# A four-layer graph network on one core: the third layer's normalisation moved from ScalarE to GpSimd and VectorE

## What is computed

```python
def _layernorm(x, axis=-1, eps=1e-05):
    m = jnp.mean(x, axis=axis, keepdims=True)
    v = jnp.var(x, axis=axis, keepdims=True)
    return (x - m) / jnp.sqrt(v + eps)
...
    h = jnp.maximum(_layernorm(x, axis=-1), 0.0)
    x = x + _L0_gnn_ref(h, adj, L0_gnn_W, L0_gnn_a)
    h = jnp.maximum(_layernorm(x, axis=-1), 0.0)
    x = x + _L1_gnn_ref(h, adj, L1_gnn_eps, L1_gnn_W1, L1_gnn_b1, L1_gnn_W2, L1_gnn_b2)
    h = jnp.maximum(_layernorm(x, axis=-1), 0.0)
    x = x + _L2_gnn_ref(h, adj, L2_gnn_weight, L2_gnn_bias)
    h = jnp.maximum(_layernorm(x, axis=-1), 0.0)
    x = x + _L3_gnn_ref(h, adj, nodemask, L3_gnn_weight, L3_gnn_w_ih, L3_gnn_w_hh, L3_gnn_b_ih, L3_gnn_b_hh)
```

## Time and profile before

| | us |
|---|---|
| median of 3 runs | 711.43 |
| lowest and highest | 709.85 and 711.65 |
| the profiled execution | 711.34 |
| its span, first to last instruction | 709.6 |
| of it, `first_layers` | about 336 |
| one steady slot | 18.02 |

### The profile page before, as it was taken

How to read it: one execution, slowest core, us unless ns; L and a number is a source line. 1 busy time by engine, 2 the same in 40 slices (tenths; PEclk the granted TensorE clock), 3 DMA queues, 4 the chain that set the end, 5 groups by cost and what they waited for, 6 DMA issues and landing times.

```text
span 709.6 us, 13197 instructions
## 1 busy us (share of the span) xinstructions
PE 659.9 (93%) x4380; PEld 430.4 (61%) x4380; DVE 601.8 (85%) x1361; ACT 524.3 (74%) x962; POOL 401.1 (57%) x356
## 2 busy tenths in 40 slices
PE   1899999999999999983899999999999999999995
PEld 1678888888888888862455555555454555555552
DVE  3677777777777787666699999999999999999996
ACT  1588888888888888732477888777777777877774
POOL 4556666666666666521255555555555555555554
PEclk9999999999999999986899999999999999999998
DMA  5111111111111100000343333333333333333332
GB/s 154 31 31 31 31 31 31 30 31 31 31 30 31 30 16 1 2 0 1 59 61 60 60 61 65 68 76 75 75 61 75 74 76 75 61 75 69 69 72 74
DMA packets 114690, 35.82 MB, mean 50 GB/s; under 512 B 87680, under 2 KB 114624, under 8 KB 114624
## 3 DMA queue, kind: packets, MB, share of 16 engines
q1 hardware_dynamic: 114624, 34.98, 23.3%
HBM read 9.80 MB, written 4.19 MB: 20 GB/s over the span
## 4 chain that ended last, share of the span: by engine, by line
DVE 36%; issue 9%; PE 3%; POOL 2%; ACT 1%; DMA 0%; DVEq 0%; POOLq 0%; SPq 0%
DVE h_parts L1286 12%; DVE cand L1293 7%; DVE t_parts L1278 6%; DVE r L1297 5%; DVE new L1282 4%; PE psum L50 3%; POOL h0T L1253 2%; DVE out L1269 2%; DVE h_parts L1288 0%; DMA h_nodes<-h_parts 0%; DVEq L1296 0%; ACT cand L1230 0%; POOLq L1035 0%; PE psum L1182 0%; ACT z L1225 0%
## 5 line engine op out<-in xcount | busy, mean ns | idle before, releaser
L50 PE MATMUL psum<-h_parts,gru_w 128*128 128x512 f16 x720 | 185.1, 382 | 6.1 <-DVE out L1269 3.6
L1253 POOL TENSOR_TENSOR h0T<-cand,zh 128x512 f32<-128x512 f32 x80 | 101.6, 1270 | 142.8 <-DVE cand L1293 142.8
L50 PE MATMUL psum<-t_parts,gru_w 128*128 128x512 f16 x720 | 181.5, 379 | 0.0
L50 PEld LDWEIGHTS psum<-h_parts,gru_w 128*128 128x128 f16 x720 | 69.9, 98 | 91.6 <-issue 10.6
L1247 POOL TENSOR_TENSOR zh<-z,h0T 128x512 f32<-128x512 f32 x80 | 101.7, 1272 | 26.2 <-ACT z L1225 26.2
L50 PEld LDWEIGHTS psum<-t_parts,gru_w 128*128 128x128 f16 x720 | 67.1, 98 | 66.2 <-DVE t_parts L1278 2.3
L1222 ACT CAST t_parts<-psum 128x512 f16<-128x512 f32 x80 | 46.8, 585 | 73.1 <-PE psum L50 73.1
L1286 DVE CAST h_parts<-h0T 128x512 f16<-128x512 f32 x80 | 90.1, 1126 | 4.8 <-PEq L373 4.8
L572 POOL TENSOR_TENSOR prob<-prob,row_max 128x512 f32<-128x512 f32 x64 | 68.7, 1087 | 19.7 <-DVE row_max L947 18.5
L1230 ACT ACTIVATE cand<-new,gates_b 128x512 f32<-128x512 f32 x80 | 65.0, 812 | 6.7 <-DVE new L1282 6.6
L913 DVE BATCH_NORM_STATS2 stats<-x_all 128x6 f32<-128x128 f32 x256 | 55.5, 279 | 13.9 <-DMA x_all<-in_x 8.9
(11 more groups left out here) (131 smaller groups left out, 1202.2 us busy)
## 6 DMA issues: line engine op xcount, KB each, us to landing
x_all<-in_x SPq DMA_DIRECT2D x16, 256.0 KB, 3.2
adj<-in_adj SPq DMA_DIRECT2D x16, 256.0 KB, 2.8
out_x<-out SPq DMA_DIRECT2D x16, 256.0 KB, 2.3
h_nodes<-h_parts SPq DMA_TRANSPOSE x80, 3.1
gw<-in_L_gnn_weight SPq DMA_DIRECT2D x1, 320.0 KB, 4.7
W<-in_L_gnn_W SPq DMA_DIRECT2D x2, 128.0 KB, 4.6
wi<-in_L_gnn_w_ih SPq DMA_DIRECT2D x1, 192.0 KB, 4.9
wh<-in_L_gnn_w_hh SPq DMA_DIRECT2D x1, 192.0 KB, 5.0
```

The costliest lines, as they stand in the source:

```text
L50: return nc.tensor.matmul(out, lhsT, rhs, start=start, stop=stop)
L1253: pool.tensor_tensor(state(now), by_graph(cand[now.s][:, :]), by_graph(zh[now.s][:, :]), ALU.add)\
```

## The change

For layer 2 the activations and the shift go. POOL gets a new function `centre`, which subtracts the mean on the whole 128x512 tile, at the very start of its slot, ahead of `add_self`. DVE gets `normalise_2` where `shift_of(at(3), 2)` stood: it waits for `centred[2]` and for `rstd_ready[2]`, and then does four `tensor_scalar` of 128x128, in place on `y[2]`, each of which multiplies by the graph's `rstd` and takes the maximum with 0. ACT still makes `rstd`. Layer 1's normalisation stays as it was under new names (`normalise_1`, `shift_of_1`).

```diff
@@ -586,11 +586,21 @@
+            def centre(group, n):
+
+                wait_apart(var_ready[n], group.count)
+                if group.before(1).exists:
+                    wait_apart(z_psum[n - 1], group.before(1).count)
+                pool.tensor_tensor(y[n][:, :, :], xs(group), mean_var[n][:, :, 0:1].to_broadcast([128, GROUP, DIM]),
+                                   ALU.subtract).then_inc(centred[n], 1)
+
             def slot(at, number):
                 if number == 1:
                     score_weights.pick_rows(pool)
                 if number == 2:
                     pool.wait_ge(gru.layers_loaded, gru.all_layers_loaded)
+                if at(3):
+                    centre(at(3), 2)
                 if at(2):
                     add_self(at(2))
                 if at(3):
...
-            def normalise(group, n):
-
-                wait_apart(shift_ready[n], group.count)
+            def normalise_1(group):
+
+                wait_apart(shift_ready, group.count)
                 for g in range(GROUP):
-                    last = a.activation(y[n][:, g, :], t["x"][:, group.graph(g), :], ACT.Relu,
-                                        bias=shift[n][:, g:g + 1], scale=rstd[n][:, g:g + 1])
-                last.then_inc(y_ready[n], 1)
+                    last = a.activation(y[1][:, g, :], t["x"][:, group.graph(g), :], ACT.Relu,
+                                        bias=shift[:, g:g + 1], scale=rstd[1][:, g:g + 1])
+                last.then_inc(y_ready[1], 1)
...
                 if at(2):
                     rstd_of(at(2), 2)
-                    normalise(at(2), 2)
                 if at(3):
                     keep_h0T(at(3))
...
+            def normalise_2(group):
+
+                dve.wait_ge(centred[2], group.count)
+                dve.wait_ge(rstd_ready[2], group.count)
+                for g in range(GROUP):
+                    last = v.tensor_scalar(y[2][:, g, :], y[2][:, g, :], rstd[2][:, g:g + 1], 0.0, ALU.mult, ALU.max)
+                last.then_inc(y_ready[2], 1)
...
                 if at(3):
-                    shift_of(at(3), 2)
+                    normalise_2(at(3))
                 if number == GROUPS + 2:
                     gru.scale(dve)
                     gru.split(dve)
```

More of the change, by code:

```diff
@@ L388, in first_layers @@
         rstd = [one(f"rstd{n}", [128, GROUP]) for n in LAYERS]
-        shift = {n: one(f"shift{n}", [128, GROUP]) for n in (1, 2)}
+        shift = one("shift", [128, GROUP])
         y = [one(f"y{n}", [128, GROUP, DIM]) for n in LAYERS]
@@ L414, in first_layers @@
         rstd_ready = [sem(f"rstd_ready{n}") for n in LAYERS]
-        shift_ready = {n: sem(f"shift_ready{n}") for n in (1, 2)}
+        shift_ready = sem("shift_ready")
         y_ready = [sem(f"y_ready{n}") for n in LAYERS]
-        centred = {n: sem(f"centred{n}") for n in (0, 3)}
+        centred = {n: sem(f"centred{n}") for n in (0, 2, 3)}
         gone_ready = sem("gone_ready")
@@ L864, in slot @@
                 if at(2):
-                    normalise(at(2), 1)
+                    normalise_1(at(2))
                 if at(1):
@@ L920, in moments, with shift_of_1 @@
                 last.then_inc(var_ready[n], 1)
[L922 to L925, removed]
+            def shift_of_1(group):
+                dve.wait_ge(rstd_ready[1], group.count)
+                v.scalar_tensor_tensor(shift[:, :], mean_var[1][:, :, 0], -1.0, rstd[1][:, :], ALU.mult, ALU.mult)\
+                    .then_inc(shift_ready, 1)
+            def normalise_2(group):
[4 more added lines that the diff above has]
+                last.then_inc(y_ready[2], 1)
             def find_gone(group):
@@ L998, in slot @@
                 if at(2):
-                    shift_of(at(2), 1)
+                    shift_of_1(at(2))
                 if at(0):
```

## The result

The changed kernel takes 748.0 us (median of 4 runs, 747.22 to 748.14) against 711.54 before: a ratio of 1.0506, with a 95% interval of 1.0489 to 1.0524. It is slower, as forecast, but by 36 us and not by 22, and it lies above the upper end of the range, 739. The profiled execution took 747.22 us, with a span of 745.4.

What follows compares the result with a forecast made beforehand. A loop of DVE's chain plus PE's own work was taken to bound the kernel; 13 steady slots x 1.54 = 20.0 us plus 1.75 at the end gave 21.8, so 733.1 us from 711.34, range 729 to 739.

Steps and rivals of the forecast that it cites:

- The bound: Steady slot: DVE's chain of 6.89 us plus PE's own 11.13 us sets its length of 18.02 us.
- ACT worth nothing: ACT's four removed activations, 1.65 us per slot, lie outside the loop and were costed at 0.
- POOL's subtraction and `add_self`: POOL's slot start: subtraction 0.27 us after bn_aggr, 1.04 long; add_self follows with 0.04 overlap, runs 1.26, ends at 194.35.
- The standstill: DVE's first scaling is blocked while POOL's add_self runs and ends 0.07 us after it, at 194.42.
- the rival in which DVE gets in between: DVE's first scaling starts as POOL's subtraction ends, so add_self waits: 0.50 us per slot, 718.0 us; chance 0.09.
- The scalings: DVE's other three scalings follow each other at 0.14 us each, 0.42 for three, between 0.08 and 0.20.
- d: Lengthening of DVE's chain, and so of each steady slot: 1.54 us, with bounds of 1.26 and 1.90.
- The clock: PE's granted clock falls in its longer pause, 1.7 us per slot; held only as a rival, chance 0.07.
- The rival's 746 us: PE's clock falling in every third slot, about 3 us each, adds some 13 us: 746 us; chance 0.07.
- The tail: Slots 16, 17 and 18 at the end add 0.8, 0.85 and 0.1 us, 1.75 together; the GRU itself is untouched.

Runs made afterwards that it cites:

- with PE filled: The changed kernel with seven added float32 matmuls of 128x128 on PE between layer 2's aggregation and the scores: 739.27 us, ratio 1.0397.
- the delayed kernel before: The kernel before with nine bn_stats of a constant tile into scratch behind the shift on DVE: 746.94 us, ratio 1.0503.
- both kernels rearranged: Changed kernel with DVE's moments ahead of the scalings and add_self behind POOL's bias, 713.28 us; kernel before with add_self behind the bias, 706.64 us.

## Why the prediction was right and where it was wrong

**The bound: right.** A loop through DVE's chain and PE's own work set the slot, with a wait of 0.18 us as its only trace. A delay put into that chain in the kernel before reproduced the loss (746.94 us), and taking the shift's standstill out of it made the kernel faster. The loop had more room in it than the row showed: 0.45 us of pause, not 0.18. The prediction's sentence "making it shorter gives back at most the 0.18" was wrong for that reason.

**ACT worth nothing: right.** Putting the activations back left the time at 748.2.

**POOL's subtraction and `add_self`: right,** to 0.01 us: the start 0.27 after the variance, 1.04 long, `add_self` right behind, the end at 0.04 less than the sum of both.

**The standstill: right.** The first scaling ended 0.09 us after `add_self` (210.62 + 1.28 = 211.90 against 211.81), where 0.07 was forecast, and it disappeared when `add_self` was moved. The Trainium skill (SBUF — State Buffer, "Who interferes with whom") has the rule that whoever issues first gets the shared ports for the whole instruction. The trace agrees in each of slots 3 to 17, where the four scalings are shown as 1.86 or 1.87 us and `add_self` starts first; the rival in which DVE gets in between did not occur in any. With POOL idle, in the kernel that moved `add_self`, the four took 0.88 us.

**The scalings: mis-sized.** The term was 0.14 from start to start; measured was 0.195 to 0.20. I had gone halfway between a `bn_stats` and a `bn_aggr`, for two numbers at a time. That is what the form with a constant takes, 0.13 to 0.14 from start to start, but a scale from SBUF adds 0.06 to each, for which there was no unblocked row. With it d is 1.74 instead of 1.54, and the steady slots lose 2.6 us more.

**The clock: the step that failed.** The sum has no term for the clock. The prediction had its fall as a rival with a chance of 0.07, and read from slot 2 that a gap of 0.93 us did not fell the clock. The new pause was twice as long, and no row of the kernel before covered it; that was no ground to hold the clock up and put the term at nothing. In place of nothing it was five falls and about 8 us, the largest part of the miss. The price of a fall was put at 3 us, from a stretch of 6.5 us at the lower level; here it stayed low for 3.4 us and cost 1.6. The rival's 746 us came near by luck: its 13 us for the clock were too many, on top of a sum that was too small elsewhere.

Across the runs the falls go with the pause. With pauses of 0.2 to 0.7 us per slot (as the rows show them) there was none, with 1.1 to 1.4 none, with 1.35 to 1.66 none, and with 1.92 to 2.29 (three kernels) there were five among the steady slots. Which slots it hits is not decided by the length of the pause: most pauses of 1.95 us had no fall, and neither had the longest, 2.29. What decides it stays open.

**The tail: too small.** The forecast had 1.75 us for slots 16 to 18 and nothing after them. The same milestones in both kernels:

| milestone | before, us | after, us | later by |
|---|---|---|---|
| scores of slot 3 | 52.32 | 54.15 | 1.83 |
| scores of slot 15 | 268.54 | 298.24 | 29.70 |
| scores of slot 16 | 286.22 | 318.38 | 32.16 |
| `add_attended` of slot 17 | 302.31 | 335.60 | 33.29 |
| first copy of the GRU's weights | 311.06 | 345.18 | 34.12 |
| first cast of the GRU | 336.49 | 371.22 | 34.73 |
| end of the span | 709.6 | 745.4 | 35.8 |

The chain is 1.83 up to slot 3's scores and 12 x 1.74 = 20.9 up to slot 15's, together 22.7. The four falls in that stretch are 6.46. Two slots without a fall, 8 and 15, are 0.28 us longer than the others, 0.56 together, and so are two slots of the kernels with `add_self` moved and with PE filled; the cause is not shown. From slot 15's scores to slot 16's it is 2.46 more, for the fifth fall and slot 16 itself. The two were not separated in this kernel. In the delayed kernel before, which had no fall there, this slot lost 0.69, and by that the fall cost about 1.8. From slot 16's scores to the GRU it is another 2.57 us. In slot 17 the transposes of the GRU's weights run at the lower clock, which they did not before. In slot 18 the scalings delay the GRU's scale operations by 1.46 us (357.83 against 322.25, less the 34.12), and with the block on the split gone 0.61 of it stays. The last 1.1 us arise within the GRU, which the change does not touch. Its start runs at the lower clock in both kernels; after its first cast that lasts about 7.5 us before and 8.7 after. At half the clock 1.2 us more cost at most 0.6, so this could be half of the 1.1 us, and it was not tried; the rest is open.

The sum then is 22.7 + 6.46 + 0.56 + 2.46 + 2.57 + 1.07 = 35.8 us, the difference of the two spans (745.4 - 709.6). Since the milestones come from the same traces, the sum must come out; what it shows is where the time went. Of the 14 us that the forecast of 21.8 lacks, about 8 are the clock, 2.6 the scalings in the steady slots, and some 3.3 the two longer slots and the tail.

## What to carry to other kernels

An engine that is busy 99% of a slot can still be waiting in a loop through another one: look for a wait that comes back in every slot with the same size, follow both engines around it, and ask which instructions stand between the release and the wait. Here work taken off an engine outside that loop gave nothing, and a wait put inside it cost its whole length in every slot. When such a wait makes TensorE pause, count the fall of its clock as a cost of its own wherever no row shows that a pause of that length leaves it up. And before a shorter instruction is looked for, look at what runs on GpSimd at that moment: here moving one GpSimd instruction by one place, with no other change, gave 5.3 us, where the exchange of work cost 36, and still 6.6 with both kernels rearranged.

## What the runs showed that I had not expected

- PE's clock fell in 5 of 13 slots that were alike, each time for 3.4 us, in three kernels with a pause of 1.9 us or more. The slots where it fell were not quite the same ones: two kernels had a fall at 216 to 218 us where the third had it at 195.7, and one had its first at 54.3 and none at 298.
- A scale read from SBUF makes a `tensor_scalar` 0.06 us longer for 128 numbers per partition (0.28 against 0.22), and by the nearest row, which writes bf16, about as much for 512.
- A pause of TensorE of 0.45 us stood in the trace as 0.18, since the ends of matmul rows are modelled and can hide idle time. The starts of the rows are the better ruler.
